# Graph-network kernel: the description of the edge tiles moves into the block that loads the weights

## The chip, the cores and the metric

The kernel runs on one core of one Trainium2 chip. The metric is the device time of one execution in microseconds; the median of three executions is compared. Five engines run their own instruction streams and meet at semaphores: TensorE (PE; PEld is its weight load), VectorE (DVE), ScalarE (ACT), GpSimd (POOL) and SyncE (SP), which only issues transfers here.

## The reference, cut to what matters

Four graph layers run one after another over 50,000 nodes of 128 features and 25,000 edges sorted by destination. Each is pre-normalised and residual:

```
h = relu(layernorm(x)); x = x + GAT5(h, edges, edge_attr_16)   # 5 attention layers, 2 heads
h = relu(layernorm(x)); x = x + HGT(h, edges, edge_type_2)      # 2 relations, 8 heads
h = relu(layernorm(x)); x = x + GCN(h, edges)
h = relu(layernorm(x)); x = x + CAT(h, edges, edge_type_4)      # 4 edge types, 4 heads
```

All four take a softmax or a sum over the edges of each destination. What that needs of the edge list alone (where a destination's run of edges begins and ends, its degree, the type masks) is computed once, ahead of the layers, and so are products of weights alone. The attention score of an edge also has a term that depends only on its 16 attributes: `edge_attr @ u`, with `u` made from the weights.

## The kernel before, in words

The program is a row of blocks. A block gives each engine its list of instructions; when all engines have ended theirs, semaphores are cleared, all engines meet at a barrier (line 83), and the next block begins. So a block costs the time of its slowest engine, and nothing of the next one overlaps it. Three blocks concern us, called in `gnn_stack`:

1. `prepare_weights` (line 93). SP issues 115 small loads one after another (line 150 in the helper `load`); PE, DVE and ACT wait for all of them (`loaded`, 16 per load). Then PE transposes weights (lines 197 to 202), DVE copies them out, PE makes the products (lines 212 to 236), and DVE writes them to kept tiles (lines 288 to 307), `K.edge_u` first. POOL sets a few constants at the start.
2. `describe_tiles` (line 756). The edges lie in 196 tiles of 128 (C = 196), two to a lane: a tile `[128, 2, 128]` holds one edge tile per partition and half. SP issues 12 loads (lines 805 to 815): 11 of integers counted by `s.loaded`, and the edge attributes `ex` counted by `s.ex_in`. POOL makes index numbers and constant masks (lines 835 to 852). DVE makes `ub` (line 859, the only early step that needs `K.edge_u`), then run masks (865 to 904), slot numbers (907 to 922), counts (925 to 932), the masks of the tile sequence `K.q` (936 to 948), `lane_c` from `K.gat_u` (951, 952), the sequence scans (956 to 959), the typed masks (962 to 977), degrees (982 to 986), small tables (988 to 1003) and the copies of turned results (1006 to 1010). Nearly every DVE instruction waits for the one before it (the helper `Order`). SP stores the masks to DRAM in 15 transfers (lines 817 to 830) and waits until all have landed. ACT and PE compute the edge values: 28 rounds of 7 tiles, each a transpose (1030), a copy by ACT (1017), a product (1035) and a copy by ACT (1019). PE's list has the 28 rounds first, then the transposes of the run ends and of the counts (1040, 1045), of the sequence result (1050) and of the degrees (1055), each behind a wait for DVE.
3. `node_pass` (line 310), which begins with SP's load of `cat_b` (line 385) and the first blocks of x.

All order inside a block is written by hand; there is no planner.

Of the kernel before, what the change touches and what calls it, by code (L numbers as in the profile page):

```python
# [92 lines left out]
def prepare_weights(nc, K, I):  # L93


    with ExitStack() as ctx:
# [32 lines left out]
        with nc.Block(no_gpsimd_drain=True) as block:  # L129
            @block.gpsimd  # L130
            def _(eng):
# [13 lines left out]
                                  base=d - 1, channel_multiplier=-1).then_inc(made, 1)  # L145

            @block.sync
            def _(eng):
                def load(out, in_):
                    eng.dma_start(out, in_).then_inc(loaded, 16)  # L150
                with nc.allow_non_contiguous_dma(reason="small weights"):
# [36 lines left out]
                    load(K.hgt_ba[:, :], I.hgt_ba.unsqueeze(0).broadcast_to([P, D]))  # L188

# [57 lines left out]
            def _(eng):  # L247
                step = Order(eng, dve_step)
                eng.wait_ge(loaded, 16 * n_loads)
# [506 lines left out]
def describe_tiles(nc, K, I):  # L756
# [7 lines left out]
    with ExitStack() as ctx:  # L764
# [27 lines left out]
        lane_h = A.sb("lane_h", [LN, 1])  # L792
        psP = [A.ps(f"psP{j}", [P, 2 * C]) for j in range(2)]
# [3 lines left out]
        s = A.sems(("loaded", "made", "step", "masked", "typed", "counted", "filled", "turned_out", "turned_back", "tiled", "degrees",  # L797
                    "degrees_turned", "mask_out", "ex_in", "ub_ready", "turned", "exT", "scored", "taken"))
        EB = GM // 2
        blocks = range(C // EB)  # L800
        with nc.Block(no_gpsimd_drain=True) as block:
            @block.sync
            def _(eng):
                with nc.allow_non_contiguous_dma(reason="tile ends"):
                    eng.dma_start(raw[:, :, :], I.dst_lane.rearrange("(h p) q -> p h q", p=P)).then_inc(s.loaded, 16)
                    eng.dma_start(around_raw[:, 0, :], I.tile_prev).then_inc(s.loaded, 16)
                    eng.dma_start(around_raw[:, 1, :], I.tile_next).then_inc(s.loaded, 16)
                    eng.dma_start(ends_raw[:, :], I.tile_ends.broadcast_to([16, 2 * C])).then_inc(s.loaded, 16)
                    eng.dma_start(first_raw[:, :], I.tile_first.broadcast_to([P, C])).then_inc(s.loaded, 16)
                    eng.dma_start(K.src_tm[:, :], I.src_tm).then_inc(s.loaded, 16)  # L810
                    eng.dma_start(K.dst_tm[:, :], I.dst_tm).then_inc(s.loaded, 16)
                    for n, (lane, tm) in enumerate(((I.type2_lane, I.type2_tm), (I.type4_lane, I.type4_tm))):
                        eng.dma_start(typ_raw[:, n, :, :], lane.rearrange("(h p) q -> p h q", p=P)).then_inc(s.loaded, 16)
                        eng.dma_start(typ_tm[:, n, :], tm).then_inc(s.loaded, 16)
                    eng.dma_start(ex[:, :, :], I.ex_tm).then_inc(s.ex_in, 16)
                eng.wait_ge(s.made, 12)
                eng.dma_start(K.row_of.rearrange("(p n) one -> p (n one)", p=P), node_rows[:, :]).then_inc(s.mask_out, 16)
                eng.wait_ge(s.masked, 1)
                for h, (a, b) in enumerate(halves(C)):
                    eng.dma_start(K.mk_dram[a:b, :], mk[0:b - a, h, :, :].rearrange("p k q -> p (k q)")).then_inc(s.mask_out, 16)  # L820
                    for _, table, _ in KINDS:
                        eng.dma_start(table[a:b, 0:3 * P], mk[0:b - a, h, 0:3, :].rearrange("p k q -> p (k q)")).then_inc(s.mask_out, 16)
                eng.wait_ge(s.masked, 2)
                for h, (a, b) in enumerate(halves(C)):
                    eng.dma_start(K.ep_dram[a:b, :], endp[0:b - a, h, :]).then_inc(s.mask_out, 16)
                eng.wait_ge(s.typed, 1)
                for h, (a, b) in enumerate(halves(C)):
                    for (types, table, _), of in zip(KINDS, mkt):
                        eng.dma_start(table[a:b, 3 * P:], of[0:b - a, h, :, :].rearrange("p k q -> p (k q)")).then_inc(s.mask_out, 16)
                    eng.dma_start(K.has_dram.rearrange("r t q -> t r q")[a:b, :, :], has_type[0:b - a, h, :, :]).then_inc(s.mask_out, 16)  # L830
                eng.wait_ge(s.mask_out, 16 * 15)

            @block.gpsimd
            def _(eng):
                eng.iota(iota_i[:, :], [[1, P]], base=0, channel_multiplier=0).then_inc(s.made, 1)
                eng.iota(number_i[:, :], [[P, 2]], base=0, channel_multiplier=1).then_inc(s.made, 1)
                eng.iota(K.slot_row_tm[:, :], [[P, C]], base=K.rows, channel_multiplier=1).then_inc(s.made, 1)
                eng.memset(ones[:, :], 1.0).then_inc(s.made, 1)
                eng.memset(mask8[:, :, :], 1.0).then_inc(s.made, 1)
                eng.memset(lane_h[:, :], 1.0).then_inc(s.made, 1)  # L840
                eng.wait_ge(s.made, 6)
                for h in range(2):
                    eng.affine_select(after[:, h, :], ones[:, :], pattern=[[1, C]], compare_op=ALU.is_ge, fill=0.0,
                                      base=-1 - h * P, channel_multiplier=-1).then_inc(s.made, 1)
                eng.affine_select(lane_h[:, :], lane_h[:, :], pattern=[[0, 1]], compare_op=ALU.is_ge, fill=0.0,
                                  base=-GM, channel_multiplier=1).then_inc(s.made, 1)
                eng.affine_select(mask8[:, :, :], mask8[:, :, :], pattern=[[-EDGE_F, 8], [0, LH]], compare_op=ALU.is_ge, fill=0.0,
                                  base=0, channel_multiplier=1).then_inc(s.made, 1)
                eng.wait_ge(s.made, 10)
                eng.affine_select(mask8[:, :, :], mask8[:, :, :], pattern=[[EDGE_F, 8], [0, LH]], compare_op=ALU.is_ge, fill=0.0,  # L850
                                  base=EDGE_F - 1, channel_multiplier=-1).then_inc(s.made, 1)
                eng.iota(node_rows[:, :], [[1, K.rows // P]], base=0, channel_multiplier=K.rows // P).then_inc(s.made, 1)

            @block.vector
            def _(eng):
                step = Order(eng, s.step)
                restart, back, cont, goes, own, in_head, in_tail = (mk[:, :, k, :] for k in range(n_mask))
                eng.wait_ge(s.made, 11)
                step(eng.tensor_tensor(ub[:, :, :], mask8[:, :, :], spread(K.edge_u[:, :], 1, 8), ALU.mult))
                eng.sem_inc(s.ub_ready, 1)  # L860
                step(eng.memset(K.half[:, :], -0.5))
                step(eng.memset(fx[:, :, :, :], 0.0))
                step(eng.memset(piece[:, :, :, :], 0.0))
                eng.wait_ge(s.loaded, 16 * 11)
                step(eng.tensor_copy(d[:, :, :], raw[:, :, :]))
                step(eng.tensor_copy(around[:, :, :], around_raw[:, :, :]))
                step(eng.tensor_copy(K.iota[:, :], iota_i[:, :]))
                step(eng.tensor_copy(number[:, :], number_i[:, :]))
                step(eng.tensor_copy(K.iota_col[:, :], number[:, 0:1]))
                step(eng.tensor_copy(ends[:, :], ends_raw[:, :]))  # L870
                step(eng.tensor_copy(first[:, :], first_raw[:, :]))
                step(eng.memset(cont[:, :, 0:1], 0.0))
                step(eng.tensor_tensor(cont[:, :, 1:P], d[:, :, 1:P], d[:, :, 0:P - 1], ALU.is_equal))
                step(eng.memset(goes[:, :, P - 1:P], 0.0))
                step(eng.tensor_copy(goes[:, :, 0:P - 1], cont[:, :, 1:P]))
                step(eng.tensor_scalar(stop[:, :, :], goes, -1.0, 1.0, ALU.mult, ALU.add))
                step(eng.tensor_scalar(restart, cont, 1.0, -FAR, ALU.subtract, ALU.mult))
                step(eng.tensor_scalar(back, goes, 1.0, -FAR, ALU.subtract, ALU.mult))
                hc, tc, slot, endq, has, last_slot = (flag[:, :, k] for k in range(6))
                step(eng.tensor_tensor(hc, d[:, :, 0], around[:, 0, :], ALU.is_equal))  # L880
                step(eng.tensor_tensor(tc, d[:, :, P - 1], around[:, 1, :], ALU.is_equal))
                for h in range(2):
                    step(eng.tensor_scalar(in_head[:, h, :], d[:, h, :], d[:, h, 0:1], hc[:, h:h + 1], ALU.is_equal, ALU.mult))
                    step(eng.tensor_scalar(in_tail[:, h, :], d[:, h, :], d[:, h, P - 1:P], tc[:, h:h + 1], ALU.is_equal, ALU.mult))
                step(eng.tensor_tensor(t0[:, :, :], stop[:, :, :], in_tail, ALU.mult))
                step(eng.tensor_tensor(closes[:, :, :], stop[:, :, :], t0[:, :, :], ALU.subtract))
# [2171 lines left out]
```

## Time and profile before

| | us |
|---|---|
| median of three executions (lowest, highest) | 6116.2 (6116.01, 6125.23) |
| the profiled execution's own time | 6123.68 |
| its span in the trace | 6121.8 |
| mean granted TensorE clock | 0.89 |

| engine | busy us | share of the span | instructions |
|---|---|---|---|
| PE | 5027.1 | 82% | 29899 |
| PEld | 4241.7 | 69% | 29899 |
| DVE | 4152.4 | 68% | 16499 |
| ACT | 3250.7 | 53% | 8537 |
| POOL | 2971.7 | 49% | 2871 |

The span is the time from the first to the last instruction in the trace; the execution's own time is 1.9 us longer. Busy shares are averages over all stages. The first two blocks above take the first 194 us of the span, about 3% of it.

### The profile page before, as it was taken

How to read it: one execution, taken by the hardware profiler on the slowest of the kernel's cores; microseconds unless marked ns; L12 is line 12 of the kernel's file. 1: busy time of each engine (PE TensorE's matmuls, PEld its weight loads, DVE VectorE, ACT ScalarE, POOL GpSimd, SP SyncE). 2: the span in 40 equal slices, each digit the busy share in tenths (PEclk: the TensorE clock that was granted, in tenths of full speed). 3: DMA queues.
4: the chain of work that ended last, by engine and by line, in shares of the span. 5: the costliest groups of instructions: out<-in, count | busy, mean ns of one | idle time of the engine just before them, and what ended most of it. 6: DMA issues, size and time to landing. Idle time of an engine off the chain costs nothing. (4 is left out here: it accounts for less than half of the span.)

```text
span 6121.8 us, 105598 instructions
## 1 busy us (share of the span) xinstructions
PE 5027.1 (82%) x29899; PEld 4241.7 (69%) x29899; DVE 4152.4 (68%) x16499; ACT 3250.7 (53%) x8537; POOL 2971.7 (49%) x2871
## 2 busy tenths in 40 slices
PE   3699999999969969969969969977696775868755
PEld 3477777777759959959959958854575665756555
DVE  2577777778856657757757757768576766847755
ACT  0577777777735525525525535534474334656500
POOL 0566666655574334334424415512463337745357
PEclk9999999999979979979979979975698777989955
DMA  1699986665545435535525525538774445955432
GB/s 37 133 212 210 210 208 210 210 202 193 191 107 117 106 68 119 110 65 116 113 59 117 119 58 121 123 101 249 194 154 90 133 139 163 248 133 108 82 84 85
DMA packets 1227632, 841.34 MB, mean 137 GB/s; under 512 B 335962, under 2 KB 1188542, under 8 KB 1226736
## 3 DMA queue, kind: packets, MB, share of 16 engines
q1 hardware_dynamic: 1150020, 706.53, 45.3%
q0 software_dynamic: 77040, 128.08, 9.8%
q8 instruction: 251, 4.11, 0.3%
q14 instruction: 321, 2.63, 0.2%
HBM read 390.57 MB, written 448.11 MB: 137 GB/s over the span
## 5 line engine op out<-in xcount | busy, mean ns | idle before, releaser
L738 POOL DMA_INDIRECT gat_G<-table,k_src_row x980 | 964.1, 984 | 841.0 <-PE gat_psE L1474 642.6
L1397 ACT ACTIVATE gat_aggT<-gat_psG 128x512 f32<-128x512 f32 x490 | 292.6, 597 | 602.8 <-PE gat_psE L1474 602.8
L1469 PE MATMUL gat_psG<-gat_S,gat_G 128*128 128x256 f32 x1960 | 597.1, 387 | 10.1 <-DVE gat_loop L1280 10.1
L1474 PE MATMUL gat_psE<-gat_S,gat_exr 128*128 128x128 f32 x3920 | 601.1, 276 | 0.0
L1274 DVE TENSOR_SCALAR gat_S<-k_iota,k_endpos,gat_al 128x128 f32<-128x128 f32 x1960 | 544.4, 340 | 19.5 <-PE gat_psE L1474 16.5
L442 POOL TENSOR_TENSOR nodes_rstd<-nodes_var,k_half 128x14 f32<-128x14 f32 x138 | 360.4, 2611 | 390.5 <-DVE nodes_var L502 385.4
L1474 PEld LDWEIGHTS gat_psE<-gat_S,gat_exr 128*128 128x128 f32 x3920 | 518.4, 193 | 0.0
L1485 PE MATMUL gat_psZ<-gat_aggT,t_gat_wh 128*128 128x256 f32 x1960 | 504.6, 380 | 1.3 <-ACT gat_hT L1404 1.3
L1471 PE MATMUL gat_psG<-k_ident,gat_loop 128*128 128x128 f32 x1960 | 376.6, 274 | 0.0
L1404 ACT ACTIVATE gat_hT<-gat_psZ,t_gat_bias 128x256 f32<-128x256 f32 x490 | 232.4, 474 | 236.1 <-PE gat_psZ L1486 236.1
L1485 PEld LDWEIGHTS gat_psZ<-gat_aggT,t_gat_wh 128*128 128x128 f32 x1960 | 334.9, 191 | 28.2 <-issue 2.1
L1389 ACT ACTIVATE gat_loop<-gat_own,gat_al 128x128 f32<-128x128 f32 x980 | 334.7, 392 | 26.9 <-DVE gat_al L1263 21.9
L1471 PEld LDWEIGHTS gat_psG<-k_ident,gat_loop 128*128 128x128 f32 x1960 | 278.2, 142 | 100.8 <-issue 2.2
L1469 PEld LDWEIGHTS gat_psG<-gat_S,gat_G 128*128 128x128 f32 x1960 | 299.7, 193 | 13.3 <-issue 10.6
L1486 PE MATMUL gat_psZ<-gat_aggE,t_gat_ewT 128*128 128x256 f32 x980 | 291.5, 379 | 0.0
L663 ACT ACTIVATE nodes_rows<-nodes_psR 128x396 f32<-128x396 f32 x528 | 268.2, 508 | 26.6 <-PE nodes_psR L583 2.2
L583 PEld LDWEIGHTS nodes_psR<-t_ident_v,nodes_hTa 128*128 128x128 f32 x1584 | 220.7, 191 | 70.7 <-issue 1.5
L583 PEld LDWEIGHTS nodes_psR<-t_ident_v,nodes_hTb 128*128 128x128 f32 x1584 | 219.8, 191 | 70.5 <-issue 0.9
L738 POOL DMA_INDIRECT cat_edge_G<-table,k_src_row x196 | 198.3, 1012 | 132.3 <-ACT cat_edge_hm L1851 90.2
L1249 DVE TENSOR_TENSOR_SCAN gat_f<-gat_mk,gat_ee 28x128 f32<-28x128 f32 x70 | 28.9, 412 | 343.5 <-ACT gat_ee L1379 343.5
L738 POOL DMA_INDIRECT nodes_xg<-in_x,first_dst_tm x196 | 196.8, 1004 | 132.5 <-POOLq L83 83.5
L1498 PEld LDWEIGHTS gat_psR<-t_ident_v,gat_hT 128*128 128x128 f32 x1568 | 236.8, 190 | 21.3 <-ACT gat_hT L1404 1.2
(650 smaller groups left out, 14499.2 us busy)
## 6 DMA issues: line engine op xcount, KB each, us to landing
table<-nodes_rows SPq DMA_DIRECT2D x660, 198.0 KB, 3.9
table<-nodes_n SPq DMA_DIRECT2D x396, 192.0 KB
gat_own<-table SPq DMA_DIRECT2D x490, 132.0 KB
table<-gat_rows SPq DMA_DIRECT2D x392, 132.0 KB
nodes_x<-in_x SPq DMA_DIRECT2D x132, 192.0 KB
out<-nodes_x_out SPq DMA_DIRECT2D x132, 192.0 KB
gat_exr<-in_ex_pad SPq DMA_DIRECT2D x70, 336.0 KB
gat_G<-table,k_src_row POOLq DMA_INDIRECT x980
```

Of the source, the lines that this page charges most:

```text
L442: eng.tensor_tensor(rstd[:, k % 3, :], var[:, k % 3, :], K.half[:, 0:M], ALU.pow).then_inc(s.pow, 1)
L583: mm = eng.matmul(psR[l % 2][:, t * ROWW:(t + 1) * ROWW], hT[:, t * P:(t + 1) * P], K.ident_v[:, l, :], start=True, stop=True)
L663: eng.activation(rows[:, l - 1, b % 2, :, :], wide(psR[l % 2], T, ROWW), ACT.Copy).then_inc(s.rows_out, 1)
L738: eng.indirect_dma_start(to, None, table, bass.IndirectOffsetOnAxis(ap=index, axis=0)).then_inc(sem, 16)
L1274: ins = eng.tensor_scalar(S[:, i % RS, t, h, :], K.iota[:, :], K.endpos[:, 2 * i + t:2 * i + t + 1], al[:, g % 2, 0, a:a + 1], ALU.is_equa ...
L1389: ins = eng.activation(loop[:, i % RS, t, 0, :], own[:, i % RO, t, 0:D], ACT.Copy, scale=al[:, g % 2, 1, a:a + 1])
L1397: eng.activation(aggT[:, i % RA, :, :, :].rearrange("p t h q -> p (t h q)"), psG[i % 2][:, :], ACT.Copy).then_inc(s.aggT, 1)
L1469: eng.matmul(o, G[:, g % RG, c, 0:D], S[:, i % RS, t, :, :].rearrange("p h q -> p (h q)"), start=True, stop=False)
L1471: eng.matmul(o[:, h * P:(h + 1) * P], loop[:, i % RS, t, h, :], K.ident[:, :], is_transpose=True, start=False, stop=(h == H - 1))
L1474: mm = eng.matmul(psE[i % 2][:, t * P:(t + 1) * P], exr[:, g % 2, c, (1 - h) * EDGE_F:(1 - h) * EDGE_F + P], S[:, i % RS, t, h, :], start= ...
L1485: eng.matmul(o, K.gat_wh[:, l, h, :], aggT[:, i % RA, :, h, :], start=(h == 0), stop=False)
L1486: eng.matmul(o, K.gat_ewT[:, l, :], aggE[:, i % RA, :, :].rearrange("p t q -> p (t q)"), start=False, stop=True).then_inc(s.mixed, 1)
```

## The change

The loads, the POOL numbers, the masks of DVE and the mask stores of `describe_tiles` become four functions. `describe_tiles` now calls `prepare_weights` itself and hands them over; there they run inside the block of the weights: the 12 loads ahead of the weights' loads on SP, the 15 stores behind them, the numbers at the end of POOL's list, the masks at the head of DVE's list. The typed masks (962 to 977), which stood behind the sequence scans, are now part of these masks. The second block keeps `ub`, `lane_c`, the sequence scans, the degrees and everything behind them on DVE, the edge values on ACT and PE, and it has no SP and no POOL list any more. On PE the transposes of run ends and counts come first, and the transpose of the sequence result stands between rounds 14 and 15 of the 28. `s.step2` counts DVE's steps in the second block. No instruction of the computation is added or dropped.

```diff
-def prepare_weights(nc, K, I):
+def prepare_weights(nc, K, I, load_tiles, store_tiles, number_tiles, mask_tiles):
...
                 eng.affine_select(in_head[:, :], in_head[:, :], pattern=[[d, HGT_HEADS]], compare_op=ALU.is_ge, fill=0.0,
                                   base=d - 1, channel_multiplier=-1).then_inc(made, 1)
+                number_tiles(eng)

             @block.sync
             def _(eng):
+                load_tiles(eng)
+
                 def load(out, in_):
...
                     load(K.hgt_ba[:, :], I.hgt_ba.unsqueeze(0).broadcast_to([P, D]))
+                store_tiles(eng)
...
             @block.vector
             def _(eng):
                 step = Order(eng, dve_step)
+                mask_tiles(eng)
                 eng.wait_ge(loaded, 16 * n_loads)
...
+        def load(eng):
+            with nc.allow_non_contiguous_dma(reason="tile ends"):
+                eng.dma_start(raw[:, :, :], I.dst_lane.rearrange("(h p) q -> p h q", p=P)).then_inc(s.loaded, 16)
...
+                eng.dma_start(ex[:, :, :], I.ex_tm).then_inc(s.ex_in, 16)
+
+        def store(eng):
+            eng.wait_ge(s.made, 12)
+            eng.dma_start(K.row_of.rearrange("(p n) one -> p (n one)", p=P), node_rows[:, :]).then_inc(s.mask_out, 16)
+            eng.wait_ge(s.masked, 1)
...
+            eng.wait_ge(s.typed, 1)
...
+            eng.wait_ge(s.mask_out, 16 * 15)
+
+
+        def numbers(eng):
+            eng.iota(iota_i[:, :], [[1, P]], base=0, channel_multiplier=0).then_inc(s.made, 1)
...
+        def masks(eng):
+            step = Order(eng, s.step)
...
+            eng.wait_ge(s.loaded, 16 * 11)
+            step(eng.tensor_copy(d[:, :, :], raw[:, :, :]))
...
+            step(eng.tensor_copy(q.valid[:, 0::2], q.ownx[:, :]))
+
+            step(eng.tensor_copy(typ[:, :, :, :], typ_raw[:, :, :, :]))
...
+            eng.sem_inc(s.typed, 1)
+
+
+        prepare_weights(nc, K, I, load, store, numbers, masks)
...
             @block.vector
             def _(eng):
-                step = Order(eng, s.step)
+                step = Order(eng, s.step2)
+                q = K.q
                 restart, back, cont, goes, own, in_head, in_tail = (mk[:, :, k, :] for k in range(n_mask))
-                eng.wait_ge(s.made, 11)
+                hc, tc, slot, endq, has, last_slot = (flag[:, :, k] for k in range(6))
                 step(eng.tensor_tensor(ub[:, :, :], mask8[:, :, :], spread(K.edge_u[:, :], 1, 8), ALU.mult))
                 eng.sem_inc(s.ub_ready, 1)
-                step(eng.memset(K.half[:, :], -0.5))
...
-                step(eng.tensor_copy(q.valid[:, 0::2], q.ownx[:, :]))
-
                 u = K.gat_u[0:LN, :, EDGE_F].rearrange("p (l h) -> p l h", h=H)
...
                 eng.sem_inc(s.filled, 1)
-
-                step(eng.tensor_copy(typ[:, :, :, :], typ_raw[:, :, :, :]))
...
-                eng.sem_inc(s.typed, 1)
 
                 eng.wait_ge(s.turned_back, 1)
...
             @block.tensor
             def _(eng):
+                def turn_back():
+                    eng.wait_ge(s.filled, 1)
+                    for h, (a, b) in enumerate(halves(C)):
+                        for e in range(2):
+                            mm = eng.transpose(psF[0:b - a, 4 * h + 2 * e:4 * h + 2 * e + 2], seq[:, 0, 2 * a + e:2 * b:2], K.ident[0:2, 0:2])
+                    mm.then_inc(s.turned_back, 1)
+
+                eng.wait_ge(s.masked, 2)
+                for k, of in enumerate((endp, node)):
+                    for h, (a, b) in enumerate(halves(C)):
+                        mm = eng.transpose(psP[0][:, k * C + a:k * C + b], of[0:b - a, h, :], K.ident[0:b - a, 0:b - a])
+                mm.then_inc(s.tiled, 1)
+                eng.wait_ge(s.counted, 1)
+                for e in range(2):
+                    for h, (a, b) in enumerate(halves(C)):
+                        mm = eng.transpose(psQ[:, e * C + a:e * C + b], piece[0:b - a, h, e, :], K.ident[0:b - a, 0:b - a])
+                mm.then_inc(s.turned_out, 1)
                 eng.wait_ge(s.ex_in, 16)
                 eng.wait_ge(s.ub_ready, 1)
                 for b in blocks:
+                    if b == len(blocks) // 2:
+                        turn_back()
                     j = b % 2
...
-                eng.wait_ge(s.masked, 2)
...
-                mm.then_inc(s.turned_back, 1)
                 eng.wait_ge(s.degrees, 1)
...
-                prepare_weights(nc, K, I)
                 describe_tiles(nc, K, I)
                 node_pass(nc, K, I, out)
```

## Rows read from the trace of the kernel before

**Rows 1.** SP in order of time: start, duration, line, transfer

```profile
0.80 0.44 SPq L150 DMA_DIRECT2D weights_w_raw<-in_gat_w  x1
...
53.78 0.43 SPq L150 DMA_DIRECT2D k_hgt_ba<-in_hgt_ba  x1
108.78 0.38 SPq L805 DMA_DIRECT2D tiles_raw<-in_dst_lane  x1
...
114.05 0.43 SPq L815 DMA_DIRECT2D tiles_ex<-in_ex_tm  x1
114.52 0.43 SPq L817 DMA_DIRECT2D row_of<-tiles_node_rows  x1
...
176.14 0.34 SPq L829 DMA_DIRECT2D hgt_masks<-tiles_mkt  x1
...
180.45 1.43 SPq L830 DMA_DIRECT2D has_type<-tiles_has_type  x1
194.36 0.36 SPq L385 DMA_DIRECT2D nodes_cat_b<-in_cat_b  x1
```

**Rows 2.** DVE in order of time: start, duration, work, in brackets the idle time before

```profile
57.22 0.16 DVE L251 TENSOR_REDUCE weights_conf_max<-weights_conf 128x1 f32<-128x5 f32 x1 [57.22 <-DMA k_hgt_ba<-in_hgt_ba]
...
107.58 0.17 DVE L307 COPY k_hgt_bq<-weights_ps_w 128x16 f32<-128x16 f32 x1
...
116.34 0.29 DVE L865 CAST tiles_d<-tiles_raw 128x256 f32<-128x256 int32 x1 [4.08 <-DMA tiles_typ_tm<-in_type_tm]
...
140.04 0.25 DVE L948 COPY k_q_valid<-k_q_ownx 16x196 f32<-16x196 f32 x1
...
163.97 0.43 DVE L962 CAST tiles_typ<-tiles_typ_raw 128x512 f32<-128x512 int32 x1
...
175.37 0.69 DVE L977 TENSOR_TENSOR tiles_has_type<-tiles_has_type,tiles_mk 128x512 f32<-128x512 f32 x1
...
186.21 0.36 DVE L1010 COPY k_own_tm<-tiles_psP 128x196 f32<-128x196 f32 x1
```

**Rows 3.** What SP waited for, 0 to 200 us: total, times, longest

```profile
SPq L801 <- DMA has_type<-tiles_has_type: 11.5, 1, 11.5
```

**Rows 4.** PE in order of time in the second block

```profile
123.00 0.46 PE L1030 MATMUL tiles_psT<-k_ident,tiles_ex 128*112 128x128 f32 x1 [16.94 <-DMA tiles_ex<-in_ex_tm]
...
158.88 0.53 PE L1040 MATMUL tiles_psP<-k_ident,tiles_endp 128*128 128x128 f32 x2
...
159.53 0.86 PE L1045 MATMUL tiles_psQ<-k_ident,tiles_piece 128*2 128x128 f32 x4
163.94 0.52 PE L1050 MATMUL tiles_psF<-k_ident,tiles_seq 2*128 2x2 f32 x4 [3.54 <-DVEq L960]
178.68 0.59 PE L1055 MATMUL tiles_psP<-k_ident,tiles_count 128*128 128x128 f32 x2 [14.22 <-DVEq L987]
179.06 0.54 PE L1055 MATMUL tiles_psP<-k_ident,tiles_mk 128*128 128x128 f32 x2
```

**Rows 5.** POOL in order of time: the last number made in the second block

```profile
111.24 0.46 POOL L852 IOTA tiles_node_rows<- 128x396 int32 x1
```

**Rows 6.** Stretches: length, PE, PEld, DVE, ACT, POOL busy, PE clock, DMA share, GB/s

```profile
12.00:54.00 42.00, 0.00 (x0) 0.00 (x0) 0.00 (x0) 0.00 (x0) 0.00 (x0) 1.00 0.08 9
...
108.00:123.00 15.00, 0.00 (x0) 0.00 (x0) 6.46 (x26) 0.00 (x0) 2.67 (x12) 1.00 0.59 182
...
73.00:90.00 17.00, 16.34 (x77) 16.35 (x77) 2.07 (x10) 0.00 (x0) 0.00 (x0) 1.00 0.00 1
```

**Rows 7.** PE groups by line: count, busy us, mean ns; 123 to 159 us, then 2000 to 2100

```profile
L1030 PE MATMUL tiles_psT<-k_ident,tiles_ex 128*112 128x128 f32 x28 | 11.8, 422 | 16.9 <-DMA tiles_ex<-in_ex_tm 16.9
...
L1471 PE MATMUL gat_psG<-k_ident,gat_loop 128*128 128x128 f32 x99 | 19.0, 273 | 0.0
```

**Rows 8.** PE groups by line, 205 to 215 us, then 235 to 245

```profile
L583 PE MATMUL nodes_psR<-t_ident_v,nodes_hTa 128*128 128x132 f32 x6 | 1.5, 427 | 0.0
...
L583 PE MATMUL nodes_psR<-t_ident_v,nodes_hTa 128*128 128x132 f32 x12 | 1.7, 276 | 0.0
```

## The prediction before the run

> **What bounds the kernel now.** I read SP's and DVE's instructions in order of time, then what SP waited for, then PE's and POOL's instructions, and last a few stretches and groups. Only the first 194 us matter: every block begins after the block before has ended on all engines, so the edit can change the start of the node pass and hardly anything behind it. In [rows 1] the reader is to see three things. SP spends 0.80 to 54.21 us issuing the weights' 115 loads, one each 0.46 us. The tiles' loads come at 108.78, only after the weights are done. The node pass's first transfer starts at 194.36. In [rows 2] DVE does nothing for 57.22 us, until the last weights' load has landed, works until 107.75 (107.58 + 0.17), and starts on the tiles at 116.34. It ends at 186.57 (186.21 + 0.36). The second block ends later than that: SP's last store is issued by 181.88, and SP then waited 11.5 us for it to land [rows 3], to 193.4. So the first block is bound by SP's issue, then by the weights' chain of PE and DVE; the second by DVE's masks, PE's 28 rounds, DVE again, and at the end by the landing of stores.
>
> **The change, part by part.**
>
> *The 12 loads, moved ahead of the weights' loads.* Line 805 starts at 108.78 and the instruction behind the twelfth load at 114.52 [rows 1]: 5.74 us of issue. All of it is on the path, since SP's issue is what the weights wait for: the last weights' load is issued 5.74 later, and DVE and PE begin at 57.22 + 5.74 = 62.96. Can it cost more? The large `ex` was issued at 114.05 and PE got it at 123.00 [rows 1, 4], 8.9 us, where the last weights' load took 57.22 - 53.78 = 3.4. If what queues behind `ex` held SP up by that difference, 5.5 us more would be lost; but the store right behind it was issued in the usual 0.43, and the 115 small loads leave 47 us in which any backlog drains. Bounds 5.74 and 11.3; I take 5.74. It can't be less, as 12 instructions are added to a queue that never pauses.
>
> Here a rule is worth weighing. From 12 to 54 us the transfers moved 9 GB/s, with a DMA share of 0.08, while SP issued without a break [rows 6]: the queue's issue is the bound, not the transfer. The Trainium skill, "DMA: Bandwidth & Descriptors", section "Issuing engines are not separate DMA queues", says that starting DMAs on several engines saves only the sequencer's time to initiate them, usually small beside the DMA itself; by it one would cost the moved loads by their bytes. That page's table ("Bandwidth") has 341 GB/s for 1 MB; the stretch 108 to 123 moved 182 GB/s for 15 us, 2.7 MB, one store among it, so an estimate by the page is 8 us, and the gain would be 2.3 us smaller.
>
> *POOL's numbers.* They end at 111.70, 2.9 us after the block's start [rows 5]. They now run from about 2.4 us and are done by 6, before the loads are in. Nothing waits behind them on POOL. Cost 0.
>
> *The masks on DVE, moved to the head of its list.* In [rows 2] they run from 116.34 to 140.29 (23.95 us), and the typed ones from 163.97 to 176.06 (12.09 us): 36.0 us. Eleven of the twelve loads, all that they wait for, were issued by 114.05 and the first mask started 2.3 later; now that point is at 0.80 + 5.27 = 6.07, so the masks run from 8.4 to 44.4. Behind them on DVE stands the wait for the weights, over at 62.96: 18.5 us of slack. The cover is DVE's idle time while SP issues. Were the masks longer than the slack, each microsecond would go straight onto the first block.
>
> *The 15 stores, behind the weights' loads on SP.* They start at 59.95, when the typed masks are long done. The last six took 17.3 us from first issue (176.14) to last landing (193.4). All fifteen at that pace take 43 us, to 103. The first block ends at 107.75 + 5.74 = 113.49 on DVE, so they are hidden with 10 us to spare even so. What is late next once the stall of 11.5 us is gone is the chain PE, DVE. A delay of the last weights' load by the stores behind it on the queue: 0 to 5.5 us (the same difference as above), taken as 0, since they are issued later.
>
> *The second block.* After the end of the first, DVE 107.75 to SP 108.78, the barrier takes 1.03 [rows 1, 2]: the block starts at 114.52. Its path is now PE:
> - the eight transposes, 158.88 to 160.39 (159.53 + 0.86): 1.51 [rows 4]; all inputs are ready;
> - 28 rounds, 123.00 to 158.88: 35.88 [rows 4]. `ub` (one small DVE instruction) and `ex` are there;
> - the four transposes of the sequence result amid them: 0.52 [rows 4]. Bounds 0 (they fit into a pause for ACT) and 1.1 (four alone at a pause each, twice the row); I take 0.52. DVE's scans take 3.54 from the counts [rows 4], against 14 rounds = 17.9 us, so PE does not wait there;
> - the transposes of the degrees, 178.68 to 179.60: 0.92 [rows 4];
> - DVE's last two copies, twice the 0.36 of [rows 2], and 0.16 for the hand-over from PE and the step between them, an estimate: 0.88.
>
> Sum: 39.71, to 154.23. Hidden beside the rounds: degrees, slots and small tables on DVE, which lie between the typed masks' end (176.06) and the last copy (186.21) [rows 2], 10.2 us, after turning back at about 134.5; so to 145, 8 us before PE's last transposes. Without that cover each microsecond beyond would count.
>
> *Barrier and node pass.* 154.23 + 1.03 = 155.26 for the transfer at 194.36 [rows 1]. **The gain is 39.1 us.** Or by blocks: the second took 194.36 - 108.78 = 85.58 us from start to start and will take 40.74; the first grows by 5.74.
>
> *The clock.* In the tiles' rounds a 128x128 matmul takes 422 ns, in the GAT loop 273 [rows 7]. I read this as the levels 1.2 and 2.4 GHz; the granted clock printed for these early stretches is 1.00, which the durations don't bear out. The node pass starts slow, 427 ns against 276 thirty microseconds later [rows 8]. It did so after PE had idled 26 us; now PE idles some 13 before it. I take the same start; if it were fast from the beginning, or slow for as long again, about 10 us of PE work would change by a third, 4 us either way.
>
> **The time.** Profiled execution 6123.7 - 39.1 = 6084.6. It was 7.5 above the median of the timed runs; from that median, 6116.2 - 39.1 = 6077.1, forecast 6077. The executions of before stand at two places, 6116 (two) and 6124 to 6125 (the third and the profiled one), so the new median can sit 9 us higher by that alone.
>
> **The rivals.**
> 1. *Issue held up behind `ex`, or the last weights late.* For: `ex` took 8.9 us to land. Against: the 0.43 right behind it. Gain 39.1 - 5.5 = 33.6, time 6083. Chance 0.08.
> 2. *The change doesn't remove the wait at the end.* If the 7.8 us between DVE's end at 186.57 and 194.36 belonged to the start of the node pass and not to the stores, 6.8 of it would stay: 6084. Against: SP's 11.5 us wait names the last store and ends at 193.4. Chance 0.04.
> 3. *The rounds run at the fast level.* PE now pauses some 3 us before them, not 17 [rows 4]. Each round holds a transpose and a product of two passes; three matmuls that shrink from 422 to 273 ns [rows 7] save at most 0.45 a round: 28 times that is 12.5, time 6065. Against: in 73 to 90 us PE was busy 16.34 of 17 us [rows 6], and the rounds behind it were at the slow duration all the same. Chance 0.04.
> The Trainium skill, "TensorE: Matmul & The Clock Gate", section "What's actually happening", holds that an idle array is throttled and that activity releases it, which would favour this rival; the busy stretch above speaks against it here.
> 4. *Slower: the node pass starts at the slow level and stays there.* Place: the node pass. Each microsecond of PE-bound work at the slow level takes 0.55 more (427/276). It cancels the gain after 39.1/0.55 = 71 us and is slower beyond 0.2% after 93; with 140 us it costs 77, time 6154. For: the start is at the slow level, and the history before it is changed. Against: thirty microseconds later the old trace is at 276, with a longer idle time before. Chance 0.03.
>
> **How the numbers follow.** The forecast has 0.78, the rivals 0.19, and 0.03 is left for a loss that I don't see and that eats most of the gain. A difference below 0.2% (12 us) can't be told from none here. Every case but the fourth and the rest is faster by more: faster 0.94, same 0.03, slower 0.03. The range goes from 6064 (rival 3) to 6094 (rival 1 or 2 with the 9 us of the upper place).
>
> **What would show it.** The first weights' load at 6.5 us; DVE masks from 8 to 44; `weights_conf_max` at 63; the last store landed before 103; DVE's `ub` near 114.6; 28 rounds of 1.28 us behind eight transposes; SP's load of `cat_b` near 155, and the distance from there to the end unchanged within 10 us. I am wrong if `conf_max` starts after 68, if SP's landing wait still ends a block, if DVE rather than PE ends the second block, or if the loss or gain lies behind the start of the node pass.

## The result, and the profile after

| | before | changed |
|---|---|---|
| median of six executions, us | 6116.1 (6112.84 to 6125.23) | 6084.02 (6075.65 to 6089.48) |
| ratio, 95% interval | | 0.9943 (0.9933 to 0.9953) |
| profiled execution, span, us | 6121.8 | 6073.8 |
| start of `cat_b`, the node pass's first transfer, us | 194.36 [rows 1] | 156.36 |

The changed kernel is faster by 0.57%, 0.47 to 0.67. 6084 lies inside the range of 6064 to 6094, 7 us above the forecast of 6077. Up to the node pass the trace gained 38.0 us, where 39.1 was forecast. The remaining 10.0 us by which the two spans differ lie behind it and are scatter, as shown below. Ratios, here and below, are not the quotients of the medians and differ a little from them (here 0.9948).

SP of the changed kernel, in order of time; this answers to [rows 1]:

```profile
6.13 0.43 SPq L815 DMA_DIRECT2D tiles_ex<-in_ex_tm  x1
6.60 0.43 SPq L153 DMA_DIRECT2D weights_w_raw<-in_gat_w  x1
...
8.08 1.01 SPq L153 DMA_DIRECT2D weights_rows<-in_gat_b  x1
9.13 3.46 SPq L153 DMA_DIRECT2D weights_ew_raw<-in_gat_ew  x5
...
62.03 0.43 SPq L153 DMA_DIRECT2D k_hgt_ba<-in_hgt_ba  x1
62.51 0.43 SPq L819 DMA_DIRECT2D row_of<-tiles_node_rows  x1
...
76.14 1.42 SPq L832 DMA_DIRECT2D has_type<-tiles_has_type  x1
156.36 0.36 SPq L390 DMA_DIRECT2D nodes_cat_b<-in_cat_b  x1
```

The twelve loads took 5.80 us, as forecast. But the weights' loads behind `ex` were not issued at the usual pace: the two rows at 8.08 and 9.13, six loads, took 4.47 us; in the kernel before these six took 2.74 (0.30 and 2.44). The last load was issued at 62.03, 8.25 us later than before, not 5.74. Not all of the 115 loads are small: `w_raw`, right behind `ex` (1568 KB), has 640 KB.

DVE of the changed kernel, in order of time; this answers to [rows 2]:

```profile
9.02 0.29 DVE L864 CAST tiles_d<-tiles_raw 128x256 f32<-128x256 int32 x1 [3.70 <-DMA tiles_typ_tm<-in_type_tm]
...
44.40 0.69 DVE L964 TENSOR_TENSOR tiles_has_type<-tiles_has_type,tiles_mk 128x512 f32<-128x512 f32 x1
65.05 0.16 DVE L256 TENSOR_REDUCE weights_conf_max<-weights_conf 128x1 f32<-128x5 f32 x1 [19.96 <-DMA k_hgt_ba<-in_hgt_ba]
...
114.51 0.17 DVE L312 COPY k_hgt_bq<-weights_ps_w 128x16 f32<-128x16 f32 x1
115.75 0.24 DVE L980 TENSOR_TENSOR tiles_ub<-tiles_mask,first_edge_u 128x80 f32<-128x80 f32 x1 [1.07 <-PEq L83]
...
144.92 0.36 DVE L1021 CAST k_node_tm<-tiles_psP 128x196 int32<-128x196 f32 x1
154.53 0.36 DVE L1023 TENSOR_SCALAR first_deg<-tiles_psP 128x196 f32<-128x196 f32 x1 [9.25 <-PE tiles_psP L1073]
154.93 0.36 DVE L1024 COPY k_own_tm<-tiles_psP 128x196 f32<-128x196 f32 x1
```

All masks run from 9.02 to 45.09, 36.1 us, in the time in which DVE used to idle, and 20 us of that idle time are left. In the second block DVE has its tables done at 145.3 (forecast 145) and waits 9.25 us for PE: the rounds are the bound. SP waited 12.8 us for its last store to land, to 90.4, 24 us before the first block's end; in [rows 3] such a wait ended the second block.

PE in the second block, as in [rows 4]:

```profile
115.75 0.56 PE L1048 MATMUL tiles_psP<-k_ident,tiles_endp 128*128 128x128 f32 x2 [2.76 <-PEq L83]
...
117.08 0.42 PE L1063 MATMUL tiles_psT<-k_ident,tiles_ex 128*112 128x128 f32 x1
...
135.14 0.53 PE L1042 MATMUL tiles_psF<-k_ident,tiles_seq 2*128 2x2 f32 x4
...
153.56 0.53 PE L1073 MATMUL tiles_psP<-k_ident,tiles_count 128*128 128x128 f32 x2
153.88 0.53 PE L1073 MATMUL tiles_psP<-k_ident,tiles_mk 128*128 128x128 f32 x2
```

Rounds and sequence transposes take 36.48 us (117.08 to 153.56); 35.88 + 0.52 = 36.40 was forecast.

### The profile page after: what moved, and what is told of

Its sections match the earlier page's. It is cut to its first block and busy times, and to the rows that moved or that the text cites. A ratio compares the mean times of both kernels' runs of the same rounds, so it can differ in the third digit from the quotient of the medians.

```text
span 6073.8 us, 105596 instructions
## 1 busy us (share of the span) xinstructions
PE 5012.8 (83%) x29899; PEld 4229.0 (70%) x29899; DVE 4147.0 (68%) x16499; ACT 3251.1 (54%) x8537; POOL 2973.7 (49%) x2871
## 3 DMA queue, kind: packets, MB, share of 16 engines
q1 hardware_dynamic: 1150020, 706.53, 45.1%
```

## The experiments

order_only, move_only, ex_last and two_queues ran on a chip on which the kernel before takes 6125.09 us, the others on two on which it takes 6456.64 and 6459.38; more on that at the end. Up to the node pass the two traces of the kernel before agree, though one comes from a faster chip than the other (`cat_b` at 194.36 and 193.95), so the start of `cat_b` is the yardstick, and ratios are to the kernel before on the same chip. Each run has one trace. The changed kernel's own two traces have `cat_b` 1.2 us apart (156.36 and 157.56), so a difference of 1 or 2 us between two runs is weak evidence. "The changed kernel" is always the one predicted on, and its `cat_b` is taken at 156.36; gains are counted from 194.36.

**order_only**, the kernel before with PE's new list:

```diff
+                eng.wait_ge(s.masked, 2)
...
+                eng.wait_ge(s.counted, 1)
...
                 for b in blocks:
+                    if b == len(blocks) // 2:
+                        turn_back()
...
-                eng.wait_ge(s.masked, 2)
...
-                mm.then_inc(s.turned_back, 1)
                 eng.wait_ge(s.degrees, 1)
```

> The kernel before with PE's new order alone (transposes of run ends and counts first, sequence result amid the rounds, degrees last); loads, numbers and masks stay in the second block. Theory: PE starts its rounds at 137.3, behind the counts, and ends them at 173.7; DVE ends at 175.5, the stores of the typed masks land at 173.5; cat_b near 176.5 against 194.36, a gain of 17.9 us of the 38. Rival: the order is worth little where the masks are still ahead of it, because rounds and masks no longer run side by side: then the gain stays under 8 us, cat_b after 186.

`cat_b` came at 175.49, a gain of 18.9 us; ratio 0.9969 (0.9958 to 0.9981). The theory holds: PE's order alone gains half as much as the whole change, even with the masks ahead of it.

**move_only**, the changed kernel with PE's old list (the same edit taken back):

> The changed kernel with PE's old order: 28 rounds first, then the transposes. Theory: the rounds end at 151.6, transposes and scans follow to 157.1, DVE's degrees, slots and tables then stand bare (10.4 us), DVE ends at 167.6, cat_b near 168.6: 12.3 us later than in the changed kernel, so the move alone gains 25.8 us of the 38. Rival: DVE's tail hides elsewhere and the order costs nothing once the masks are moved: cat_b near 156.

`cat_b` at 172.08, ratio 0.9959 (0.9946 to 0.9971): a gain of 22.3 us against 25.8 expected, and 15.7 later than the changed kernel against 12.3. DVE in this run:

```profile
67.33 0.16 DVE L256 TENSOR_REDUCE weights_conf_max<-weights_conf 128x1 f32<-128x5 f32 x1 [22.54 <-DMA k_hgt_ba<-in_hgt_ba]
...
160.65 0.35 DVE L996 COPY tiles_fx<-tiles_psF 128x4 f32<-128x4 f32 x2 [0.68 <-PE tiles_psF L1064]
...
170.65 0.36 DVE L1024 COPY k_own_tm<-tiles_psP 128x196 f32<-128x196 f32 x1
```

The tables stand bare, 10.4 us from 160.65 to 171.01, as the theory has it. The rest of the difference is in the first block: `conf_max` at 67.33, 2.3 later than in the changed kernel, though no instruction ahead of it differs. The last load was issued 1.0 later (63.05) and took 4.3 us to its use, not 3.0. Order alone (18.9) and move alone (22.3) together are 3 us more than the whole change, so the two gains overlap: each part removes some of the wait that the other would.

**typed_early**, the kernel before with one block of lines moved:

```diff
+                step(eng.tensor_copy(typ[:, :, :, :], typ_raw[:, :, :, :]))
...
+                eng.sem_inc(s.typed, 1)
+
                 eng.wait_ge(s.turned_out, 1)
...
-                step(eng.tensor_copy(typ[:, :, :, :], typ_raw[:, :, :, :]))
...
-                eng.sem_inc(s.typed, 1)
```

> The kernel before with one move on DVE: the typed masks (12.1 us) go ahead of the wait for PE's turned counts, in which DVE idled 19.8 us. Everything else as before. Theory: the end of the second block was set by the landing of the typed stores and by DVE's work piled up behind PE's rounds; both come 12 us earlier: typed masks ready at 152.8, their stores landed by 170, DVE done near 174.8, SP's wait for a landing shrinks from 11.5 to a few us that end before DVE, cat_b near 175.9 against 194.36, gain 18.5 us. Rival: the 7.8 us between DVE's end and cat_b belong to the start of the node pass, not to the stores: then they stay and cat_b comes at 182.6.

`cat_b` at 174.91, a gain of 19.5; ratio 0.9953 (0.9936 to 0.997). DVE's last instruction, and `cat_b`:

```profile
173.47 0.36 DVE L1011 COPY k_own_tm<-tiles_psP 128x196 f32<-128x196 f32 x1
```

```profile
174.91 0.36 SPq L385 DMA_DIRECT2D nodes_cat_b<-in_cat_b  x1
```

DVE ended at 173.83 and `cat_b` followed 1.08 later; SP's wait for the landing was as long as ever, 11.6 us, but ended at 170.5. So of the 7.8 us at the end of the second block all but 1.1 were the stores' landing, and the prediction's second rival is out. The 19.5 us are the 12.1 of the masks and some 7 of that landing. Moving twelve microseconds of masks into an idle stretch of the same engine gains as much as half of what the whole change does. Whether it would add to PE's new order wasn't run.

**ex_last** and **ex_after_landing**, the changed kernel with `ex` behind the weights' loads; the second with the last line too:

```diff
-                eng.dma_start(ex[:, :, :], I.ex_tm).then_inc(s.ex_in, 16)
...
         def store(eng):
+            eng.dma_start(ex[:, :, :], I.ex_tm).then_inc(s.ex_in, 16)
...
+                eng.wait_ge(loaded, 16 * n_loads)
                 store_tiles(eng)
```

> The changed kernel with one move: the load of ex (1568 KB) goes behind the weights' loads instead of ahead of them. In the changed kernel the weights' last load was issued at 62.03 us, 2.5 us later than 12 loads at the usual pace explain. Theory: the slip is SP held up behind the bytes of ex; then without ex ahead the weights' last load is issued at 53.78 + 5.33 = 59.1, conf_max starts near 62.5, cat_b is issued near 153.7 (2.7 us earlier than the 156.36 of the changed kernel). Rival: the slip comes with the number of loads or from the other eleven; then only the one issue of 0.47 us is saved and cat_b stays near 155.9. Total about 1 to 3 us below the changed kernel, within its scatter.

SP and then DVE of ex_last, in order of time:

```profile
7.82 2.44 SPq L153 DMA_DIRECT2D weights_ew_raw<-in_gat_ew  x5
...
59.33 0.43 SPq L153 DMA_DIRECT2D k_hgt_ba<-in_hgt_ba  x1
59.80 0.43 SPq L817 DMA_DIRECT2D tiles_ex<-in_ex_tm  x1
```

```profile
64.30 0.16 DVE L256 TENSOR_REDUCE weights_conf_max<-weights_conf 128x1 f32<-128x5 f32 x1 [19.63 <-DMA k_hgt_ba<-in_hgt_ba]
```

SP's pace is back to 2.44 for the five loads, and the last load is issued at 59.33: the slip did come from `ex`. Yet `cat_b` came at 156.19, 0.2 us earlier and not 2.7 (ratio 0.9934, 0.9916 to 0.9952). The last load now took 5.0 us from issue to use, not 3.0. The theory was half right.

> As ex_last, and SP waits for the landing of all weights' loads before it issues ex and the stores. With ex_last SP's last weights' load was issued at 59.33, 2.7 us earlier than in the changed kernel, yet conf_max came at 64.30, 5.0 after it instead of 3.0. Theory: what is issued right behind the last loads (ex and stores) slows their landing; with the wait conf_max comes 3.0 after the issue, near 62.4, all stores still land before the block ends (62.4 + 17 + some 15, near 100), ex is in by 75, and cat_b comes near 154.2. Rival: the landing takes 5 us for another reason (the time of the last loads does not depend on what follows): conf_max stays at 64.3 and cat_b near 156.

`conf_max` came at 62.70, 3.3 us after the last issue, and `cat_b` at 154.25, on the expected 154.2; ratio 0.9938 (0.9922 to 0.9955). So a large transfer ahead holds up SP's issue. That what is issued right behind also delays the landing of the last loads fits 5.0 against 3.3 us, but is less sure: with stores alone behind them the last loads took 3.0 (changed kernel, changed_again) and 4.3 us (move_only), and the run moved `ex` and the stores together. The ratios of the changed kernel, ex_last and ex_after_landing (0.9941 to 0.9943, 0.9934 and 0.9938) can't be told apart; the 2 us stand in the traces alone.

**two_queues**, the changed kernel with 51 loads on ACT's queue:

```diff
             @block.scalar
             def _(eng):
+                def load(out, in_):
+                    eng.dma_start(out, in_).then_inc(loaded, 16)
+                eng.wait_ge(made, 2)
...
+                    load(K.hgt_ba[:, :], I.hgt_ba.unsqueeze(0).broadcast_to([P, D]))
                 eng.wait_ge(loaded, 16 * n_loads)
```

> The changed kernel with the weights' last 51 loads (the 40 of att_blk and all behind them) issued by ACT, which idles there, and the other 64 by SP. Theory: the first block is bound by the issue of one queue, 0.46 us a load; SP ends its loads at 38.4 and ACT at about 25, the last lands near 41.4, and DVE's masks (45.1) become the bound: conf_max at 45.1, cat_b near 136.4, 20 us earlier than in the changed kernel, time near 6064. Rival: both queues share what makes a transfer ready (the 16 DMA engines or whatever feeds them), so the loads of the two together take as long as of one: conf_max stays near 65 and cat_b near 156.

`cat_b` at 136.06, expected 136.4; time 6060.89, ratio 0.9904 (0.9887 to 0.9921). DVE went from its last mask into the weights' work:

```profile
43.99 0.69 DVE L968 TENSOR_TENSOR tiles_has_type<-tiles_has_type,tiles_mk 128x512 f32<-128x512 f32 x1
44.90 0.16 DVE L260 TENSOR_REDUCE weights_conf_max<-weights_conf 128x1 f32<-128x5 f32 x1 [0.22 <-DVE tiles_has_type L968]
```

The first block was bound by one queue's issue. The rule of the Trainium skill ("DMA: Bandwidth & Descriptors", "Issuing engines are not separate DMA queues") that several issuing engines save only the sequencer's time holds to the letter, but that time is not small here: it was worth 20 us.

**types_between**, two_queues with 16 more loads on ACT and the typed masks moved into DVE's wait for PE's products:

```diff
+                type_tiles(eng)
                 eng.wait_ge(mixed, 1)
```

> The two-queue kernel with 16 more loads (p_col) on ACT, and the typed masks moved on DVE from ahead of the weights' work into its wait of 26.8 us for PE's products. Theory: now neither DVE's masks (33 us without the typed ones) nor one queue's issue is ahead of the weights; the last load lands near 37, conf_max at 37.3, typed masks run 54.5 to 66.6 and cost nothing, the typed stores land near 84, the block ends on DVE near 86.8, cat_b near 128.5, against 136.06 with two queues alone, time near 6053. Rival: the typed stores, now issued 22 us later, land after DVE has ended and set the end of the block again: SP's wait for a landing ends it and cat_b stays at 131 or later.

`cat_b` at 136.20: nothing gained over two_queues (ratio 0.9915, 0.9896 to 0.9934), and not by the rival either. The typed masks cost nothing, as expected (DVE still idles 14.57 us before `edge_u`), and the stores landed at 91.6, ahead of DVE's end at 94.49. What failed was the start. ACT's last load, and then DVE's first use:

```profile
36.72 0.47 ACTq L228 DMA_DIRECT2D k_hgt_ba<-in_hgt_ba  x1
```

```profile
44.65 0.16 DVE L263 TENSOR_REDUCE weights_conf_max<-weights_conf 128x1 f32<-128x5 f32 x1 [11.32 <-DMA k_hgt_ba<-in_hgt_ba]
```

The load was issued at 36.72 and DVE could begin only 7.9 us later, while SP had issued `row_of` and the mask stores from 33.04 on.

**rounds_overlap**, types_between with overlapped rounds (PE's list; ACT copies `exT` of round b ahead of the scores of round b - 1):

```diff
+                turn(0)
                 for b in blocks:
...
+                    if b + 1 < len(blocks):
+                        turn(b + 1)
                     eng.wait_ge(s.exT, b + 1)
```

> The previous kernel (types_between) with the 28 rounds overlapped: PE issues the transpose of round b+1 ahead of the product of round b, and ACT copies exT of round b before the scores of round b-1. Theory: a round took 1.28 us because transpose, copy and product of one round stand in a chain; overlapped it is PE's own time, 0.42 + 0.5, so 0.95 us a round, the rounds take 26.6 instead of 35.8, and as DVE's tables still end earlier, cat_b comes 9.2 us earlier, near 119.3, time near 6044. Rival: DVE's degrees and tables, hidden in the rounds' second half, come out: then less than 5 us are gained and DVE's last two copies follow its tables without idle time.

`cat_b` at 112.44, 23.8 us earlier than types_between; ratio 0.9887 (0.987 to 0.9904). From the second block's first instruction to `cat_b` it is 23.26 us instead of 40.64: 17.4, where 9.2 was expected. PE in the second block, types_between and then rounds_overlap (lines, count, busy us, mean ns, idle before):

```profile
L1079 PE MATMUL tiles_psU<-tiles_ub,tiles_exT 112*128 112x70 f32 x56 | 19.6, 453 | 10.3 <-ACT tiles_exT L1042 10.3
```

```profile
L1090 PE MATMUL tiles_psU<-tiles_ub,tiles_exT 112*128 112x70 f32 x56 | 17.4, 414 | 0.2 <-ACT tiles_exT L1048 0.2
```

Two rounds of rounds_overlap, in order of time:

```profile
94.35 0.42 PE L1077 MATMUL tiles_psT<-k_ident,tiles_ex 128*112 128x128 f32 x1
94.57 0.54 PE L1090 MATMUL tiles_psU<-tiles_ub,tiles_exT 112*128 112x70 f32 x2
94.90 0.42 PE L1077 MATMUL tiles_psT<-k_ident,tiles_ex 128*112 128x128 f32 x1
95.14 0.70 PE L1090 MATMUL tiles_psU<-tiles_ub,tiles_exT 112*128 112x70 f32 x2
95.63 0.42 PE L1077 MATMUL tiles_psT<-k_ident,tiles_ex 128*112 128x128 f32 x1
```

The waits for ACT are gone, 10.3 to 0.2, and the ends of matmuls now overlap the next ones. I had summed durations (0.42 + 0.5, for 0.95 a round), but the starts stand closer: two rounds take 1.28 us, 0.64 each. The rounds with the sequence transposes take 19.11 us (90.51 to 109.62), where the changed kernel's took 36.48. The other 6.4 us are the first block: `conf_max` came 4.4 earlier (the last load took 4.6 us to use instead of 7.9), and the weights' chain was 2.0 shorter.

**all_four**: rounds_overlap with `ex` and the stores behind the landing of the loads, and 8 of the `p_col` loads back on SP, so that the two queues end closer together.

> rounds_overlap with three more steps: ex goes behind the weights' loads; SP waits until these have landed before it issues ex and the stores; 8 of the p_col loads go back to SP, so both queues end their loads near 32. In types_between and rounds_overlap the last weights' load took 7.9 and 4.6 us from issue to use because SP's stores were already running; ex_after_landing had 3.3. Theory: conf_max comes at 35.5 (masks are done at 33), DVE ends the first block at 83.4, the typed stores land at 82, cat_b near 107.7 against 112.4 in rounds_overlap; about 87 us earlier than in the kernel before, time 86 us below it on the same chip. Rival: stores that now start later land after DVE's end and set the block's end: cat_b stays at 111 or later.

DVE, in order of time:

```profile
34.30 0.16 DVE L266 TENSOR_REDUCE weights_conf_max<-weights_conf 128x1 f32<-128x5 f32 x1 [1.58 <-DMA weights_skip_rep<-in_hgt_skip]
...
84.37 0.17 DVE L323 COPY k_hgt_bq<-weights_ps_w 128x16 f32<-128x16 f32 x1
...
107.42 0.36 DVE L1038 COPY k_own_tm<-tiles_psP 128x196 f32<-128x196 f32 x1
```

`cat_b` at 108.88, 1.2 later than expected, 85.1 us earlier than in the kernel before on the same chip; time 6380.94 against 6459.38, ratio 0.9867 (0.9849 to 0.9886). The changed kernel has 0.9941 there. This version beats both. What each of its steps over rounds_overlap is worth wasn't measured.

**changed_again** and **before_again**, both kernels unchanged, on the same chip.

> The changed kernel, unchanged, for a second trace. In the first pair of traces the changed kernel gained 38.0 us up to cat_b and 10.0 us more behind it, while the timed medians differ by 32. Theory: what lies behind cat_b is scatter of single executions (where TensorE's clock happens to change level), so here cat_b comes at 156.4 within 1.5 us again and the rest, cat_b to the end, may differ by up to 10 us either way from the first trace on the same chip. Rival: the change itself speeds up something behind cat_b; then the rest is again shorter than in the trace of the kernel before by about 10 us.

> The kernel before, unchanged, for a second trace on the same chip as the changed kernel's. Theory: cat_b at 194.4 within 1.5 us; the stretch behind it differs from the changed kernel's by less than 10 us and without a fixed sign; the timed medians differ by 38 us within their scatter. Rival: the stretch behind cat_b is longer than in the changed kernel by 10 us again.

`cat_b` at 157.56 and at 193.95, spans 6425.3 and 6454.5: 36.4 us gained ahead of the node pass and 29.2 in the whole span, so 7.2 were lost behind `cat_b`, where the first pair had gained 10.0. The medians are 6423.93 and 6458.2, ratio of the changed kernel 0.9941 (0.9924 to 0.9957); the kernel before against itself 1.0001 (0.9991 to 1.0012). The sign turned, so the 10 us behind `cat_b` are no effect of the change that could be relied on. In the first pair the changed kernel's trace is of its fastest execution (6075.65) and that of the kernel before of a slow one (6123.68).

## Why the prediction was right

The path was right: what ends each block, what hides under what, and that PE's rounds are the bound once the masks are gone. That the gain up to `cat_b` came within 1.1 us is in part luck: a term of 2.5 us was missed, and 1.3 us of scatter between single executions (0.4 and 0.9 in the sum below) made up for half of it. The second pair of traces, with 36.4 us, came 2.7 below.

- *The 12 loads.* The step's own term was right (5.74, measured 5.80); what was mis-sized is the hold-up behind `ex`, taken as 0 with a bound of 5.5. It measured 2.5 us of issue (3.2 in changed_again), of which 0.4 came back in the landing (3.0 us instead of 3.4; the four traces with the block of before have 3.0 to 3.4, so this is scatter). The first rival was real, at under half its price in this trace. Its estimate by bytes, 2.3 us less gain, came near in size, but it spreads the cost over all the moved loads, where ex_last puts it at `ex`. The prediction argued from one store's 0.43 us behind `ex`; the slip shows only some four loads later, and 115 loads at a steady pace never win back what the queue lost.
- *POOL, masks, stores.* As said: masks 9.0 to 45.1 (8.4 to 44.4), last store landed at 90.4 (before 103). That the stores don't disturb the last loads held in the changed kernel (3.0 us from issue to use) but not in general: it was 4.3 us in move_only, 5.0 in ex_last, where `ex` stood there too, and 7.9 in types_between, where the stores ran while ACT still issued loads.
- *The weights' chain*, taken as unchanged, was 0.9 us shorter, from `conf_max` to DVE's end 49.63 instead of 50.53. Line 206's five transposes took 0.71 us where they took 1.27 (line 202 there), as if PE had come to the fast level by then. It isn't the change: order_only has the first block of the kernel before and took 0.71 and 49.84, and move_only, with the changed kernel's first block, 1.05 and 50.32. I put these 0.9 us to the clock, by the durations alone.
- *The second block.* From DVE's end in the first to `cat_b` 41.68 us, forecast 41.77.
- *Sum:* 39.1 - 2.5 + 0.4 + 0.9 + 0.1 = 38.0.
- *Rivals.* The wait at the end went with the stores (typed_early). The rounds stayed at the slow level, 422 ns for a transpose; the trace of the changed kernel has the clock's record for this stretch, and it says so too. (So has before_again: 0.50 from 120 to 160 us, where the first trace of the kernel before printed 1.00.) The node pass left the slow level as before, some 10 us after PE's first matmul in it:

```profile
81.00:98.00 17.00, 17.00 (x81) 17.00 (x81) 1.12 (x5) 0.00 (x0) 0.00 (x0) 0.50 0.11 44
...
116.00:153.00 37.00, 26.82 (x94) 17.57 (x93) 12.04 (x36) 13.60 (x55) 0.00 (x0) 0.50 0.00 1
...
165.00:175.00 10.00, 6.58 (x21) 4.70 (x22) 1.87 (x13) 3.94 (x12) 8.59 (x7) 0.50 0.12 41
175.00:185.00 10.00, 8.84 (x44) 6.45 (x44) 1.90 (x13) 7.16 (x16) 8.45 (x7) 0.87 0.42 124
```

(Stretches of the changed kernel: length, PE, PEld, DVE, ACT, POOL busy, granted clock, DMA share, GB/s.) In the first PE was busy all the time and held 0.50, which is 1.2 GHz. By the Trainium skill, "TensorE: Matmul & The Clock Gate", "What's actually happening", so busy an engine should have been released; the rows disagree, and the measurement decides. The rows show no more than this: PE's busy time is modelled in part, and no run tells what the clock counts as activity.
- *The median.* It fell by 32.1 us, not 38 or 39; the interval of the ratio, 28.7 to 41.0 us, holds both. Six executions of one kernel spread over 12 to 14 us on either side. The forecast of 6077 was a gain taken from a trace and subtracted from a median, and it could not be held to better than that.

## What to carry to other kernels

Ahead of a barrier, ask for each engine what it waits for and until when; a chain of small vector work that needs only early data belongs into the idle time under a long row of small loads, and the pieces of one engine's list should be ordered by who waits for them, which here gained 18.9 us, half as much as the whole change, without any move between blocks. A row of small transfers costs the issue time of its queue: splitting it over two queues gained 20 us here and is worth trying first. Keep large transfers from ahead of it, which cost 2.5 us or more here; behind it they may cost too. When two engines hand a tile back and forth, put the next round's first step ahead of this round's last.

## What the runs showed of the hardware

- A load of 1568 KB (with one of 640 KB right behind it) holds up the queue, though not at once: over the whole row of weights' loads 2.5 us in the changed kernel, 3.2 in changed_again and 3.5 in move_only; 0.2 in ex_last. In two_queues, with ACT's queue beside it, SP lost 4.4 us, and in all_four, with `ex` behind the loads, 0.3.
- Two queues issue at the same time and at the same usual pace: ACT's issued its first 10 loads in two_queues in 4.69 us, one each 0.47, SP's pace is one each 0.46. But `ex`, issued by SP at 6.14, held up ACT too: six of its loads from 5.63 on took 3.99 us. In all_four, with `ex` behind the loads, seven from 5.62 on took 3.41.
- The scatter of single executions goes with the mean granted clock: among the changed kernel's six runs 6075.65 us had 0.884 and the two of 6089 had 0.881. An estimate: 0.003 of the mean clock is 37 us more at the slow level, and each such microsecond of PE-bound work costs 0.35 (1 - 276/427), some 13 us. Whether the clock sets the time or longer idle stretches set the clock isn't settled. The printed mean is not exact: the stretch ahead of a trace's first clock record counts as 1.00, whatever it was, which lasts beyond 210 us in the kernel before (mean 0.89) and to about 73 in the changed kernel.
- The kernel before took 6116 us beside the changed kernel and 6125 on the chip of order_only, but 6457 and 6459 on two others, 5.5% more. The stretch from 400 to 1200 us moved 210 GB/s with PE busy 752 us in the first trace, 185 GB/s and 702 us on a slower chip:

```profile
400.00:1200.00 800.00, 751.99 (x4787) 600.78 (x4786) 627.37 (x2499) 636.34 (x1597) 529.42 (x416) 1.00 0.83 210
```

```profile
400.00:1200.00 800.00, 702.32 (x4224) 530.62 (x4225) 552.07 (x2202) 563.76 (x1410) 468.28 (x367) 1.00 0.71 185
```

The first row is of the kernel before, the second of before_again. Up to the node pass they agree within 0.4 us. Why the transfers are slower there, and whether it is the chip itself, is open.
